# Weighted one-hots of a relational graph layer: eight fused instructions against four broadcast ones

## The reference

```python
# block 0
h = x @ W_lin + b_lin
aggr = segment_sum(h[dst] + edge_attr @ W_edge + b_edge, src)
x = layernorm(x + relu(aggr))
# block 1: three relational layers, relu behind the first two
def rgcn_conv(x, src, dst, etype, W, root, bias):
    msg = x[src]
    seg = dst * r + etype
    sums = segment_sum(msg, seg, n * r)
    cnt = segment_sum(ones, seg, n * r)
    h = (sums / maximum(cnt, 1.0)[:, None]).reshape(n, r, -1)
    return einsum('nrf,rfo->no', h, W) + x @ root + bias
x = layernorm(x + rgcn_conv(relu(rgcn_conv(relu(rgcn_conv(x))))))
```

## Time and profile before

| what | us |
|---|---|
| median of 3 runs (lowest, highest) | 5557.07 (5554.59, 5563.17) |
| span of the profiled execution, first to last instruction | 5556.6 |
| busy: POOL, PE, DVE, ACT | 4003.2, 2850.8, 2253.8, 902.5 |
| gathers of the three relational layers: first start, last start | 2351.5, 5521.0 |

### The profile page before, as it was taken

How to read it: one execution, slowest core, us unless ns; L and a number is a source line. 1 busy time by engine, 2 the same in 40 slices (tenths; PEclk the granted TensorE clock), 3 DMA queues, 4 the chain that set the end, 5 groups by cost and what they waited for, 6 DMA issues and landing times. The chain is left out here.

```text
span 5556.6 us, 69405 instructions
## 1 busy us (share of the span) xinstructions
PE 2850.8 (51%) x13859; PEld 2282.1 (41%) x13860; DVE 2253.8 (41%) x7794; ACT 902.5 (16%) x2878; POOL 4003.2 (72%) x4114
## 2 busy tenths in 40 slices
PE   2577777766677667743333336333333363333332
PEld 1244444436667667533333334333333343333332
DVE  8667777766556665522222222222222222222222
ACT  0255555541111111400000002000000020000000
POOL 3777777777777777377777774777777747777775
PEclk8788888888877776855555557555556575555555
DMA  1111111123332333422221224221222231212123
GB/s 42 48 49 47 47 47 49 47 70 79 77 79 77 79 79 77 113 53 52 52 53 52 52 52 122 53 52 52 52 52 52 51 123 52 52 52 52 52 52 51
DMA packets 268429, 340.00 MB, mean 61 GB/s; under 512 B 173603, under 2 KB 180437, under 8 KB 268398
## 3 DMA queue, kind: packets, MB, share of 16 engines
q0 software_dynamic: 129280, 239.82, 17.1%
q1 hardware_dynamic: 139118, 99.82, 6.2%
HBM read 269.80 MB, written 69.57 MB: 61 GB/s over the span
## 5 line engine op out<-in xcount | busy, mean ns | idle before, releaser
L627 PE MATMUL ps<-in_win 128*128 128x404 f16 (+1 forms) x6368 | 1278.6, 377 | 1238.4 <-DMA in_win<-y_table,idx_st 955.5
L1048 DVE TENSOR_SCALAR in_win<-iota,slot_lo,slot_w 128x128 f32<-128x128 f32 x2424 | 651.6, 369 | 2359.9 <-PE ps L627 2353.3
L627 PEld LDWEIGHTS ps<-in_win 128*128 128x128 f16 (+1 forms) x6368 | 925.4, 191 | 1594.4 <-issue 1077.5
L474 POOL DMA_INDIRECT in_win<-y_table,idx_st x1224 | 1160.1, 948 | 405.4 <-issue 366.5
L434 POOL DMA_INDIRECT slot_rows<-stage,row_st x784 | 880.4, 1123 | 263.2 <-issue 238.3
L445 POOL DMA_INDIRECT in_win<-in_x_dram,idx_st x608 | 590.9, 972 | 191.9 <-issue 182.3
L474 POOL DMA_INDIRECT more_rows<-y_table,idx_st x600 | 568.8, 948 | 182.8 <-issue 182.5
L474 POOL DMA_INDIRECT last_slots<-y_table,idx_st x600 | 568.8, 948 | 182.8 <-issue 182.5
L627 PE MATMUL ps<-more_rows,in_win 128*128 128x128 f32 x1200 | 280.0, 427 | 481.1 <-DMA more_rows<-y_table,idx_st 481.1
L488 ACT ACTIVATE idx_st<-slot_row 128x8 int32 (+1 forms) x303 | 62.2, 208 | 2849.6 <-DMA in_win<-y_table,idx_st 1436.1
L627 PE MATMUL ps<-last_slots,in_win 128*128 128x128 f32 x1200 | 280.1, 427 | 467.9 <-DMA last_slots<-y_table,idx_st 467.9
(11 more groups left out here) (161 smaller groups left out, 2609.3 us busy)
## 6 DMA issues: line engine op xcount, KB each, us to landing
in_win<-slot_rows SPq DMA_DIRECT2D x76, 268.0 KB
y_table<-in_win SPq DMA_DIRECT2D x39, 512.0 KB, 2.6
in_win<-y_table,idx_st POOLq DMA_INDIRECT x1224, 2.5
ea_in<-in_edge_attr_dram SPq DMA_DIRECT2D x54, 256.0 KB
slot_rows<-stage,row_st POOLq DMA_INDIRECT x784
ea_in<-in_edge_attr_dram SPq DMA_DIRECT2D x44, 224.0 KB
in_win<-in_x_dram,idx_st POOLq DMA_INDIRECT x608
last_slots<-y_table,idx_st POOLq DMA_INDIRECT x600, 2.5
```

The costliest lines, as they stand in the source:

```text
L474: nc.gpsimd.indirect_dma_start(out=rows[b][:, k, :], out_offset=None, in_=y_table[l], in_offset=bass.IndirectOffsetOnAxis(ap=idx_st[:, b, ...
L627: return nc.tensor.matmul(o, a, b, start=False, stop=False, skip_group_check=True)
L1048: m = v.tensor_scalar(sel_f[:, par, k, :], iota[:, 0:P], slot_lo[:, ds(i * CH + k, 1)], slot_w[:, ds(i * CH + k, 1)], ALU.is_equal, ALU.mult)
```

## The change

Only `weighted_one_hots` changes, and one semaphore, `l_half_picked`, is added. For each chunk, instead of 8 `tensor_scalar` of 128 columns, 4 `tensor_tensor` of 512 columns are issued: two compares (iota, repeated 4 times, with 4 columns of `slot_lo`, each repeated 128 times), one for each half of the chunk, and then two products in place (`sel_f` times 4 columns of `slot_w`, repeated in the same way). Each compare raises `l_half_picked`; each product waits for the compare of its half.

```diff
                 def weighted_one_hots(i, par, n):
                     dve.wait_ge(S["l_chunk_used"], i + (l * TC + NB - 1))
-                    for k in range(CH):
-                        m = v.tensor_scalar(sel_f[:, par, k, :], iota[:, 0:P], slot_lo[:, ds(i * CH + k, 1)],
-                                            slot_w[:, ds(i * CH + k, 1)], ALU.is_equal, ALU.mult)
+                    for half in range(2):
+                        at = ds(i * CH + 4 * half, 4)
+                        v.tensor_tensor(sel_f[:, par, 4 * half:4 * half + 4, :],
+                                        iota[:, 0:P].unsqueeze(1).to_broadcast([P, 4, P]),
+                                        slot_lo[:, at].unsqueeze(2).to_broadcast([P, 4, P]), ALU.is_equal
+                                        ).then_inc(S["l_half_picked"], 1)
+                    for half in range(2):
+                        at = ds(i * CH + 4 * half, 4)
+                        dve.wait_ge(S["l_half_picked"], 2 * i + (2 * l * TC + half + 1))
+                        m = v.tensor_tensor(sel_f[:, par, 4 * half:4 * half + 4, :],
+                                            sel_f[:, par, 4 * half:4 * half + 4, :],
+                                            slot_w[:, at].unsqueeze(2).to_broadcast([P, 4, P]), ALU.mult)
                     m.then_inc(S["l_sel_made"], 1)
```

More of the change, by code:

```diff
@@ L234, in gnn_resnorm @@
                  "hT_kept root_staged root_added y_made y_taken_act y_taken_dve l_idx_made l_sel_made "
-                 "l_chunk_used out_made out_in")
+                 "l_chunk_used l_half_picked out_made out_in")
         S = {n: sem(n) for n in names.split()}
```

## The result

The median of four runs is 5625.07 us (5622.88 to 5628.34), against 5556.73 us for the kernel before on the same chip. The ratio is 1.0122, with a 95% interval of 1.0108 to 1.0136: slower by 68 us. The profiled execution has a span of 5621.1 us, 64.5 us more than before's.

The account below looks back on a forecast made before the run. POOL's beat of gathers was taken to bound the layers. Held gathers +85 us, removed cost -7, DVE work 0 and waits 0 gave +78 on 5556.6: 5635 us, range 5595 to 5685.

Parts of the forecast that it names:

- The bound: Relational layers: POOL's gathers set the time, eight make 10.0 us per chunk; each layer would get about 28 us longer.
- DVE's work: One-hots in the layers: 2.5 us per chunk against 2.2, 91 us more DVE busy time, costed at nothing.
- The waits: In the new one-hots, each product's wait for its compare should be over when reached: 0 us.
- Rival (a): In the layers, waits make the fourth TENSOR_TENSOR 0.2 us late, holding a second gather 0.15 us: 45 us, 5680; chance 8%.
- The hold: In the layers, a gather meeting the second TENSOR_TENSOR is held until 1.167 us into the train: 276 x 0.31 = 85 us.
- The prediction's bounds: First TENSOR_TENSOR in the layers 0.1 us earlier: +51 us, 5608; 0.1 us later: +106, 5663; evenly spread phase: 61 us, 5618.
- What was removed: What the old one-hots of L1048 cost the layers' gathers, 2424 x (948 - 945 ns) = 7 us, goes away.
- (b): Not slower: the layers' gathers fall into free spots at TENSOR_TENSOR boundaries; -7 us, 5550; chance 4%.
- (c): The products or compares hold no gather in the layers, so only the 7 us go away: 5550; chance 2%.
- (e): The phases between gathers and one-hots in the layers scatter: 5618 us; chance 10%.
- (d): A gather in the layers is held to the end of the whole train: 417 - 7 us, 5967; chance 1%.

## Why the prediction was right

The forecast was 5635 us, within 5595 to 5685; measured were 5625. Step by step:

- **The bound.** POOL's beat of gathers sets a layer, and it did: the time from the first to the last gather of the three layers grew by 67.6 us, each layer's by 22 to 23 where the forecast had about 28, and nothing else by more than 3.
- **DVE's work.** 4 instructions of 0.69 us, 0.60 apart, from L966 and L972: the trace has 688 and 685 ns, 1.29 us for two, 1.21 to the third. DVE's busy time grew by 105 us instead of 91. It was costed at nothing, and PE waits for no one-hots at L627.
- **The waits.** 0, and L1056 has no idle time in front. Rival (a), a stretched train, did not come.
- **The hold.** This term was right in mechanism and a little too large: 276 gathers by 0.31 us were 85 us, and it was 295 by 0.26, 77. More gathers paid, and each paid less, and the two errors partly cancel. The phase came out at 0.91 instead of 0.86, mostly because the new compare starts 0.54 us after PE's last matmul starts (median), where the old one needed 0.585. The prediction had taken the old start over.
- **How firm the size was.** The prediction's bounds price 0.1 us of phase at 28 us for the whole kernel. For one gather this holds. For the kernel the copies in front of the train speak against it: however the phases came out, the total stayed within 15 us. So that the total lies within 10 us of the forecast is in part luck; it does not show that the phase was known that well.
- **What was removed.** 7 us over the median of 945 ns. Over the 944 ns that the 77.8 us above are counted from it is 9.5, and 77.8 - 9.5 = 68.3 us is what the gathers took more. With iota in PSUM the fused instructions give back 5 us in the gathers' time and 10 in the median of the runs.
- **The rivals.** (b) is excluded by the phases, (c) by the timelines of iota in PSUM, (e) by 295 of 300 trains in one band. (d), given 1%, was wrong for a chunk in mid-layer and right for the first gather of two layers, 2.4 us in all. The prediction had no term for these.

The sentence of the Trainium skill that speaks for the hold (SBUF — State Buffer, Who interferes with whom: two SBUF inputs contend with a GpSimd instruction that reads SBUF) agrees with what happens to the gathers in every run here; the end of the hold is 0.12 us before that of the instruction. That the later one blocks goes one way only in these traces: of the DVE instructions in the kernel after, 317 start while an undisturbed gather runs, like the compare at 3008.97, and take 693 ns at the median, against 685 for the rest. The one behind rival (c), that `tensor_tensor` did not stall DMAs, does not carry over to these gathers: 0.85 us into the train of the kernel after, one takes 1.27 us instead of 0.94.

## What to carry to other kernels

Where gathers issued by POOL are the beat of a stage, count for every DVE instruction beside them how many inputs it reads from SBUF, before counting instructions: an instruction that DVE has time for can still hold POOL. Reading one small input from PSUM took the hold away. The constant one cost DVE no time; the weights, which change with the chunk, cost a copy of 0.17 us in each, about 30 us of DVE's idle time in all. With the compares alone moved, the loss stayed, in the products. A stage of the same kernel that already runs the new form is a good source for such a price. A phase read from the old trace is less so: what each gather pays follows from it, but the phase moves with everything in the loop, PE's clock included.

## What the runs showed that was not expected

- A gather that is the first after a wait can be held across back-to-back TENSOR_TENSOR, although each boundary lets a gather in a running beat through: 2.13 us with two products to go, 4.53 us with six instructions, 2.53 us (128 columns copied) with a compare and two products. What makes the first one different was not found.
- Two TENSOR_TENSOR of 512 columns with one input in PSUM took 1.27 to 1.29 us, no longer than with both in SBUF.
- Within one chunk PE's granted clock can change level: in the chunks with short PE time the matmuls start 213 ns apart and the last one or two 111 ns behind the one before, the lower and the upper level of 1.2 and 2.4 GHz. The mean granted clock of layer 1 went from 0.59 to 0.67 although PE does the same work; it brought nothing, since POOL sets the beat.
